# Decoder of a two-layer transformer step: gathers, joins and first norm of a batch four ticks later, x4 two ticks later

## The reference

```
x = _layernorm(x + _L0_ffn_ref(...))    # x3 plus two weighted expert rows per token -> x4
x = _layernorm(x + _L1_attn_ref(...))   # 16 heads of 8, rotary q and k, causal softmax -> x5
```

## Time and profile before

| what | value |
|---|---|
| time before, median of 3 runs (lowest, highest) | 1313.2 us (1311.42, 1314.19) |
| profiled execution, its own time / its span | 1302.04 us / 1299.2 us |
| PE busy in the span | 1125.1 us, 87% |
| DVE busy | 979.8 us, 75% |
| ACT busy | 849.1 us, 65% |
| POOL busy | 596.7 us, 46% |
| the decoder in the span | about 753 to 1057 us |

### The profile page before, as it was taken

One profiled execution on the slowest core, in us unless ns is written; L12 is line 12 of the kernel. 1 busy time (PEld: TensorE's weight loads), 2 busy tenths in 40 slices (PEclk: granted clock), 3 DMA queues, 4 the chain that ended last, 5 costly groups with the idle time before them and its releaser, 6 DMA issues. The chain is left out here.

```text
span 1299.2 us, 32418 instructions
## 1 busy us (share of the span) xinstructions
PE 1125.1 (87%) x10463; PEld 844.3 (65%) x10463; DVE 979.8 (75%) x3177; ACT 849.1 (65%) x2535; POOL 596.7 (46%) x901
## 2 busy tenths in 40 slices
PE   3888899999999998986299969999999979998796
PEld 2566666767676766654199955556555556777796
DVE  4577988989898998876555558898889865666365
ACT  1787788888888888764155526667667654543463
POOL 2232433353536363334544466556555212556277
PEclk9899999999999999998599989999999999999898
DMA  6100000010101000001233322114000000001672
GB/s 225 44 14 10 14 16 18 23 30 18 31 17 34 12 27 10 20 15 32 65 86 93 85 54 95 38 26 100 24 24 14 2 3 1 18 19 46 179 209 83
DMA packets 70739, 60.75 MB, mean 47 GB/s; under 512 B 10398, under 2 KB 61090, under 8 KB 70192
## 3 DMA queue, kind: packets, MB, share of 16 engines
q1 hardware_dynamic: 62048, 42.73, 11.5%
q0 software_dynamic: 6368, 12.63, 3.2%
q10 hardware_dynamic: 2160, 3.34, 0.8%
HBM read 42.36 MB, written 16.75 MB: 45 GB/s over the span
## 5 line engine op out<-in xcount | busy, mean ns | idle before, releaser
L826 PE MATMUL e_bank_turned<-c_matrices,e_probs 128*128 128x128 f32 x1024 | 161.7, 281 | 24.5 <-ACT e_probs_t L1017 22.5
L1017 ACT ACTIVATE e_probs_t<-e_bank_turned 128x512 f32<-128x512 f32 x256 | 154.8, 605 | 42.1 <-PE e_bank_turned L826 41.2
L756 POOL TENSOR_TENSOR e_rstd<-e_var_eps,c_minus_half 128x1 f32<-128x1 f32 x128 | 70.8, 576 | 217.8 <-DVE e_var_eps L1112 217.6
L826 PEld LDWEIGHTS e_bank_turned<-c_matrices,e_probs 128*128 128x128 f32 x1024 | 113.7, 142 | 66.0 <-issue 60.7
L1213 DVE TENSOR_REDUCE e_neg_max<-e_bank_scores 128x4 f32<-128x512 f32 x160 | 109.5, 684 | 37.0 <-PE e_bank_scores L877 36.3
L1038 ACT ACTIVATE e_probs<-e_scores,e_neg_max 128x128 f32<-128x128 f32 x384 | 124.2, 417 | 5.7 <-DVE e_neg_max L1244 5.2
L1861 ACT ACTIVATE d_probs_t<-d_bank_turned 128x512 f32<-128x512 f32 x128 | 78.8, 615 | 60.2 <-PE d_bank_turned L1732 60.2
L759 POOL TENSOR_TENSOR e_k_by_place<-e_q_k_k,c_matrices 128x512 f32<-128x512 f32 x64 | 66.5, 1039 | 81.8 <-DVE e_q_k_k L1253 75.5
L1033 ACT ACTIVATE e_probs<-e_scores 128x512 f32<-128x512 f32 x128 | 81.2, 634 | 33.0 <-DVE e_scores L1241 32.5
L836 PE MATMUL e_bank_mix<-e_probs_t,e_values 128*32 128x128 f32 x2048 | 81.1, 280 | 19.6 <-ACT e_probs_t L1017 19.6
L1241 DVE TENSOR_TENSOR e_scores<-e_bank_scores,e_neg_max 128x512 f32<-128x512 f32 x128 | 88.1, 689 | 3.0
(11 more groups left out here) (326 smaller groups left out, 3214.9 us busy)
## 6 DMA issues: line engine op xcount, KB each, us to landing
streamed<-in_s_up SPq DMA_DIRECT2D x35, 258.0 KB, 3.1
sorted_rows<-scratch_sorted SPq DMA_DIRECT2D x71, 64.0 KB, 1.8
scratch_expert_out<-m_y SPq DMA_DIRECT2D x71, 64.0 KB, 1.6
sorted_rows<-scratch_sorted SPq DMA_DIRECT2D x39, 65.0 KB, 2.7
up<-in_m_up SPq DMA_DIRECT2D x1, 2064.0 KB, 7.8
e_xT<-in_xT SPq DMA_DIRECT2D x32, 64.0 KB, 1.9
e_x_in<-in_x SPq DMA_DIRECT2D x32, 64.0 KB, 2.1
e_ctxT<-in_ctxT SPq DMA_DIRECT2D x32, 64.0 KB, 1.9
```

The source lines that it names most:

```text
L756: nc.gpsimd.tensor_tensor(rstd[slot][:], ve[slot][:], c["minus_half"][:, 0:1], ALU.pow).then_inc(rstd_ready[kind], 1)
L826: last = nc.tensor.transpose(turned_bank[:, j * P:(j + 1) * P], pr[k % 3][:, j, :], c["ident"][:])
L1017: nc.scalar.activation(pt[k % 4][:], turned_bank[:], ACT.Copy).then_inc(probs_t_ready, 1)
```

## The change

Offsets of steps in `phase_decode` are changed; no instruction is added or removed but for six products of constants.

- gather -25 to -21, join with its statistics -17 to -13, `rstd` of x4 -17 to -13, and the POOL drains that stand ahead of two gathers -26 to -22: four ticks later, all together.
- x4 -13 to -11 on DVE, `x4_bo` -13 to -10 on POOL.
- the loops start at tick -21 instead of -25, and the constant products at -15 instead of -21, which leaves 5 instead of 11 of them ahead of the first turned x4.

```
--- before.py
+++ after.py
@@ -1641,7 +1641,7 @@
                                                             sem("rstd5_ready"))
         links, buffers_set, first_squared = sem("links"), sem("buffers_set"), sem("first_squared")
         block = ctx.enter_context(nc.Block(no_gpsimd_drain=True))
-        FIRST, LAST = -25, UNITS_ALL + 21
+        FIRST, LAST = -21, UNITS_ALL + 21
         TICKS = range(FIRST, LAST)
 
         @block.sync
@@ -1684,18 +1684,18 @@
                     pool.wait_ge(var5_ready, b + 1)
                     nc.gpsimd.tensor_tensor(rstd[4 + b % 4][:], ve[4 + b % 4][:], c["minus_half"][:, 0:1], ALU.pow)\
                         .then_inc(rstd5_ready, 1)
-                if (b := due(tick, -13)) is not None:
+                if (b := due(tick, -10)) is not None:
                     pool.wait_ge(x4_ready, b + 1)
                     if b >= 7:
                         pool.wait_ge(joined5, b - 6)
                     nc.gpsimd.tensor_tensor(x4_bo[b % 7][:], x4[b % 2][:], c["l_bo"][:], ALU.add).then_inc(x4_bo_ready, 1)
-                if (b := due(tick, -17)) is not None:
+                if (b := due(tick, -13)) is not None:
                     pool.wait_ge(var4_ready, b + 1)
                     nc.gpsimd.tensor_tensor(rstd[b % 4][:], ve[b % 4][:], c["minus_half"][:, 0:1], ALU.pow)\
                         .then_inc(rstd4_ready, 1)
-                if (b := due(tick, -26)) is not None and b in (12, 22):
+                if (b := due(tick, -22)) is not None and b in (12, 22):
                     pool.drain()
-                if (b := due(tick, -25)) is not None:
+                if (b := due(tick, -21)) is not None:
                     gather(b)
                 if tick == 104:
                     pool.drain()
@@ -1816,7 +1816,7 @@
                     for k in range(G):
                         last = nc.tensor.transpose(vec_bank[:, k * P:(k + 1) * P], ot[n % 2][:, k * P:(k + 1) * P], c["ident"][:])
                     last.then_inc(mix_back, 1)
-                if -21 <= tick < -4:
+                if -15 <= tick < -4:
                     stream(nc, c, turned_bank[:, 0:2 * P])
                 if tick == UNITS_ALL + 4:
                     pe.wait_ge(probs_t_ready, UNITS_ALL)
@@ -1897,7 +1897,7 @@
                         dve.wait_ge(rotated, b - 1)
                     nc.vector.tensor_tensor(halves[b % 2][:], vec_bank[:].rearrange("p (a u) -> p a u", u=P), c["rope"][:],
                                             ALU.mult).then_inc(halves_ready, 1)
-                fifth, fourth = due(tick, 11), due(tick, -17)
+                fifth, fourth = due(tick, 11), due(tick, -13)
                 if fourth is not None:
                     b = fourth
                     dve.wait_ge(x3_loaded[b % 4], (b // 4) * 16 + 16)
@@ -1942,7 +1942,7 @@
                     nc.vector.scalar_tensor_tensor(
                         out=sub4[b % 2][:], in0=y[1][b % 4][:], scalar=route["weights"][:, b, 1:2], in1=sub4[b % 2][:],
                         op0=ALU.mult, op1=ALU.add).then_inc(joined4, 1)
-                if (b := due(tick, -13)) is not None:
+                if (b := due(tick, -11)) is not None:
                     dve.wait_ge(rstd4_ready, b + 1)
                     if b >= 2:
                         dve.wait_ge(x4_bo_ready, b - 1)
```

## The result

| | before | after |
|---|---|---|
| median | 1312.31 us (1310.89 to 1314.19, 4 runs) | 1326.09 us (1322.54 to 1328.92, 4 runs) |
| profiled execution, its own time / its span | 1302.04 / 1299.2 us | 1328.92 / 1327.2 us |

The ratio is 1.0095, 95% interval [1.0075, 1.0114]: 13.8 us slower. I had forecast slower, by 3.5 us, and a range that ended at 1320.5. The direction holds, the size does not.

What follows compares the result with a forecast made beforehand. PE was nearest to a bound, with DVE on the batch's path in ticks 1 and 2. -1.4 + 0.26 + 4.6 = +3.5 us on 1313.2 gave 1316.7 us, range 1311 to 1320.5.

Steps and rivals of the forecast that it cites:

- The batch (27 x 0.17 = 4.6 us): Decoder batches 2 to 28: x4 in DVE's full tick 1 lengthens each from 8.74 to 8.91 us, +4.6 us.
- The 0.26 of batch 1: Decoder batch 1: ACT has no mixT to copy yet, so x4's full 0.26 us on DVE is added.
- Absorbed: Rival, chance 0.20: slack in tick 1 takes up x4, only the fill's -1.4 us counts, 1311.8 us.
- A lighter tick 3 that pays: Rival, chance 0.10: DVE's lighter tick 3 saves up to 0.14 us a batch, 5.2 us with the fill, 1308 us.
- Contention with POOL: Rival, chance 0.13: no slack, and x4 beside POOL's rotation costs 0.07 us more a batch; +7.8 us, 1321 us.
- The fill (-1.4 us): Decoder start: first scores 1.9 us sooner, less a wait of batch 3's x4 for its `rstd`; 1.4 us kept.
- PE's clock in the fill: Rival, chance 0.05: PE, idle before the first scores, falls to 1.2 GHz and loses some 2 us; +5.5, 1318.7 us.
- The sum: Whole kernel: -1.4 + 0.26 + 4.6 = +3.5 us, profiled execution from 1302.04 to 1305.5 us.
- The step that failed: Whole kernel: the 11.2 us between profiled execution and timed median carried along unchanged, giving a median of 1316.7 us.
- the ring of the batch: Decoder batch, reciprocal to reciprocal in 8.74 us: DVE's tick 1 and 2 work, ACT's exponential and mixT copy, then PE.
- From there DVE is never idle until its join: Ring step, DVE after the reciprocal's release: `halves`, then the maximum of bank 2 and its subtraction follow without idle time.
- `x4_bo` on POOL gives room in tick 3: POOL, decoder: moving `x4_bo` frees time in tick 3, its result is read 20 ticks later; costed at nothing.

Runs made afterwards that it cites:

- a2: The kernel after, unchanged, run again on another chip: 1302.30 us against 1300.72 for the kernel before, ratio 1.0012.
- c2: The kernel before with x4 alone moved to -11 and `x4_bo` to -9, gathers and joins unmoved: 1303.56 us against 1299.51, ratio 1.0030.
- e1: The kernel after with the constant products from tick -21 on again, six more: first scores at 16.22 us instead of 15.57.
- a4: The kernel after, unchanged, run again on another chip: 1301.52 us against 1298.79 for the kernel before, ratio 1.0018.
- a3: The kernel after, unchanged, run again on another chip: 1304.32 us against 1299.21 for the kernel before, ratio 1.0030.
- c1: The kernel after with `x4_bo` moved from -10 to -9, back in tick 3: 1301.57 us against 1299.51 for the kernel before, ratio 1.0013.
- g1: The kernel after with x4 of batches from 4 on at -12, in DVE's idle tick 0, and `x4_bo` at -9: 1297.21 us against 1300.72 before, 0.9983.

## Why the prediction was right and wrong

**The batch (27 x 0.17 = 4.6 us): right.** In a2 the distance from `halves` to the maximum of bank 2 and PE's wait for the copy are those forecast, 0.86 us (905.25 to 906.11) and 0.36:

```profile
905.25 0.69 DVE L1898 TENSOR_TENSOR d_halves<-d_bank_vec,c_rope 128x512 f32<-128x512 f32 x1
...
905.86 0.34 DVE L1950 TENSOR_SCALAR d_x<-d_sub,d_mean_var,d_rstd 128x128 f32<-128x128 f32 x1
...
906.11 0.69 DVE L1882 TENSOR_REDUCE d_neg_max<-d_bank_scores 128x4 f32<-128x512 f32 x1
...
908.49 0.30 PE L1794 MATMUL d_bank_act<-c_matrices,d_x 128*128 128x128 f32 x1 [0.35 <-ACT d_mixT L1850]
```

DVE's wait ahead of the reciprocal is 0.91 us, where I had 1.1. Batch 8.90 instead of 8.91; 4.1 to 4.6 us between the first and the last reciprocal, where the term gave 4.6. The 0.26 of batch 1 falls ahead of the first reciprocal, and c2, where x4 moves and the gathers stay, shows it: its lead over the kernel before shrinks from 0.63 us at the maximum of bank 3 of batch 0 to 0.37 at the first reciprocal, by 0.26.

**The rivals of this term.** Absorbed: c2 has the term alone and pays 4.15 us. A lighter tick 3 that pays: in c2 it is as light, and the batch is 8.90.

**Contention with POOL (0.07 us a batch in the upper bound): absent in the middle, and its row was misread.** x4 takes 0.34 us at 905.86, as in tick 3, though `q_k_rotated` starts beside it at 906.03. The x4 of 0.41 us (773.02) did not run beside POOL's arithmetic: in the trace of before POOL's `rstd` ended at 772.99 and its next instruction, a gather, started at 773.17. In the fill of a2 two x4 in the same position took 0.41 us as well, but a third (758.89) took 0.35; what makes the difference is not shown.

**The fill (-1.4 us): right in size.** The first scores came 1.75 us sooner (forecast 1.9), 0.65 of it by the six products that are gone (e1) and the rest by POOL's order. Then x4 of batch 3 waited for its `rstd`:

```profile
767.65 0.41 DVE L1950 TENSOR_SCALAR d_x<-d_sub,d_mean_var,d_rstd 128x128 f32<-128x128 f32 x1 [1.66 <-POOL d_rstd L1694]
...
772.90 0.41 DVE L1950 TENSOR_SCALAR d_x<-d_sub,d_mean_var,d_rstd 128x128 f32<-128x128 f32 x1 [0.72 <-POOL d_rstd L1694]
773.23 0.68 DVE L1882 TENSOR_REDUCE d_neg_max<-d_bank_scores 128x4 f32<-128x512 f32 x1
```

0.72 us of wait where I had about 1, and the maximum of bank 2 at 773.23. The decoder started 1.88 us earlier in this trace (752.79 against 754.67), so that is 775.11 in the terms of the prediction, which said 775.1. What the table keeps at the first reciprocal is 1.1 us: 1.4 less the 0.26 of batch 1.

**PE's clock in the fill: it does fall, sometimes, and costs nothing.** The table by stretch of a2; the granted clock is the third number from the end:

```profile
770.00:772.00 2.00, 2.00 (x11) 1.82 (x11) 1.97 (x4) 1.52 (x5) 1.90 (x4) 0.50 0.17 47
```

and of a4, the same kernel and stretch:

```profile
770.00:772.00 2.00, 1.32 (x12) 1.13 (x12) 1.97 (x4) 1.35 (x5) 1.90 (x3) 1.00 0.23 63
```

In a2 the granted clock went down to 0.50, the lower level of 1.2 GHz (in a3 to 0.53 on average over the same 2 us); PE had stood idle 2.62 us before the turn of batch 2, at 768.11. In a4 it stayed at 1.00, with 2.09 us idle at the same place, and in the result's trace too, with 2.43. The first reciprocal came after 34.83, 34.86 and 34.83 us: the products that ran at half speed were those of a later batch, off the path. I had put this rival at +2 us, and had called a clock that falls before 775 a sign that I am wrong: it fell, and it was no such sign.

**The sum: right on three chips, wrong in the result.** Between first gather and last reciprocal the kernel after took 3.0, 3.5 and 3.0 us more than before (forecast 3.5; of before there is one trace), and the three ratios are 1.0012, 1.0030 and 1.0018, where 3.5 us are 1.0027. The gathers, joins and drains that I costed at nothing did cost nothing there.

**The step that failed** is the one after the sum: "The timed median lies 11.2 us above that execution; the same difference on 1313.2 gives 1316.7 us." I took those 11.2 us for an offset that the change would carry along. They were a symptom of a condition in which the change costs more. The kernel before takes 1299 to 1301 us on the four chips of my runs and 1312.3 in the runs of the result. The profile of before, at 1302.04, shows none of the late signals; it is of the kind of the four, and I read the ring of the batch from it.

In the ring two steps did not hold in that condition. "From there DVE is never idle until its join": `halves` waited 0.57 us a batch for the signal of L1774 (10.8 us in 19). And "`x4_bo` on POOL gives room in tick 3" was put at nothing: the room lets the gathers start 0.6 us earlier, over PE's q and k products. With that the signal of the last L1774 falls due (0.29 us after the matmul's start, as in the other traces) 0.85 us after the start of the second gather instead of 0.27. In the result's trace 40 of 47 of PE's signals that fell due 0.8 to 1.0 us after the start of a POOL transfer were late, and 2 of 65 that fell due in its first 0.3 us.

The sizes fit. Outside the decoder the result's trace is 13.0 us longer than a2 (11.8 up to the first gather, 1.2 after the last reciprocal), and the median of before is 11.6 to 13.5 us above those of my runs, so the decoder before seems to have lost nothing there; the decoder after lost 13.7 us more than in a2 (315.98 - 302.29). The traced execution was the slowest of its four, 2.8 us above the median. The result's 13.8 us are thus a common part of some 3 us and some 11 that exist only in that condition.

**What stays open.** That in the condition of the result the place of the gathers decides is read from one trace and not shown by an experiment. For it: the last late signal of L1774 (1027.75) is the last with a gather ahead of it, and the batches behind it that have an x4 and no gather take 8.90 us; a batch whose second gather started 0.47 us ahead of the last L1774 (819.34) had its signal on time, and those at 0.55 to 0.65 had it late. The kernel before was never traced in that condition. The deciding experiment, c1 and after side by side in it, was tried on two more chips, and neither showed it. What the condition is I do not know, nor why a POOL transfer should hold a signal of PE. Nor do I know what c1 or g1 would do in it: their signals fall due 0.43 and 0.65 us after the start of the second gather, and of those due between 0.3 and 0.8 us 43 of 119 were late.

## What to carry to other kernels

Before a difference is carried from a profiled execution to a timed median, ask whether they agree: three runs within 2.8 us of each other and a profiled one 11 us below them may not be of one kind, and a schedule that is tight in one may be loose in the other. When a result is far from a sum whose steps all show up in the trace, run the same kernel again on another chip before building theories on its edits; that one run settled more than four variants. An instruction that must move costs nothing only where its engine waits, and the timeline names the place: x4 in the wait of tick 0 instead of the full tick 1 was worth 4.1 us (267.46 to 263.35).

## What the runs showed of the hardware

- The same program, with its instructions in the same places, had PE's completion signal 0.29 us after the start of the last q and k product on three chips (0.43 in the one batch of the fill that ran at a granted clock of 0.50) and, from the batch at 847 to that at 980 us, 0.80 to 0.95 us after it in the result's trace. The row of the matmul at full clock reads 0.28 us in all of them. Only the start of the waiting instruction and the event on the semaphore show it.
- In the result's trace 129 of 142 late signals of PE arrived 1.35 to 1.7 us after the start of an indirect transfer on POOL. In before, a2, a3 and a4, with the same transfers, none did.
- The granted clock fell from 1.00 to 0.50 some 17 us after the decoder's first gather in two of the four traced executions of one kernel and not in the other two (2.62 and 2.61, then 2.43 and 2.09 us of idle PE ahead of the same turn). The idle time varies by half a microsecond from run to run, and with it, it seems, whether the clock falls.
- The kernel before took 1299.5, 1300.7, 1299.2 and 1298.8 us (medians) on four chips, and 1312.3 us in the runs of the result: 1% between chips or their conditions, as much as the whole effect in question.
